# Out-projection as four more outputs of the second feed-forward's program

## The reference, cut to what matters

```
xn = _layernorm(x)                                       # x is the first layer's result
x = x + attn(xn) + ffn(xn)
# attn: 16 heads of 32
out = softmax(causal(q @ k.T / sqrt(32))) @ v            # before: o_parked, not yet divided by the sums
out = out.reshape(b, l, d) @ W_out.T + b_out
# ffn
h = silu(xn @ w_gate) * (xn @ w_up)                      # 2048 wide
h_sparse = of each four neighbours the two largest by magnitude, the others 0
return h_sparse @ w_down
```

## Time and profile before

| | us |
|---|---|
| median of 3 runs | 1831.02 (1829.15 to 1831.48) |
| the profiled execution | 1828.41 |
| its span | 1826.6 |
| PE busy | 1721.3 (94%) |
| DVE busy | 1052.3 (58%) |
| POOL busy | 242.9 (13%) |
| mean granted clock of PE | 0.975 |

### The profile page before, as it was taken

The page is one execution under the profiler, slowest core; times in us unless marked ns, Lnnn a source line. Parts: engine busy times, 40 slices in busy tenths (PEclk is TensorE's granted clock), DMA queues, the critical chain, the costliest instruction groups (busy, mean ns, idle before and its releaser), DMA issues. The chain is left out here.

```text
span 1826.6 us, 24866 instructions
## 1 busy us (share of the span) xinstructions
PE 1721.3 (94%) x8428; PEld 1383.6 (76%) x8428; DVE 1052.3 (58%) x1800; ACT 748.2 (41%) x1548; POOL 242.9 (13%) x200
## 2 busy tenths in 40 slices
PE   6999999999999989979998999948899999999997
PEld 4767877878878768857776777737688888888885
DVE  4422556455423532569997999946457556555653
ACT  4412223223113422269998999932322212222121
POOL 3001202101200030200000000036203203203200
PEclk9999999999999989989999999979899999999998
DMA  7200211110100149623454444272201100101011
GB/s 282 91 9 0 70 35 47 29 41 24 35 18 35 46 181 282 253 85 103 122 134 136 128 122 123 60 244 70 93 1 35 35 1 35 34 0 34 11 46 46
DMA packets 63434, 145.12 MB, mean 79 GB/s; under 512 B 8153, under 2 KB 16729, under 8 KB 61666
## 3 DMA queue, kind: packets, MB, share of 16 engines
q1 hardware_dynamic: 63330, 143.84, 24.8%
HBM read 97.67 MB, written 46.14 MB: 79 GB/s over the span
## 5 line engine op out<-in xcount | busy, mean ns | idle before, releaser
L1781 DVE TENSOR_TENSOR pt_lo<-p_turn,pt_hi 128x512 fp32r<-128x512 f32 (+3 forms) x384 | 201.3, 551 | 25.1 <-ACT pt_hi L1756 17.7
L1774 DVE TENSOR_REDUCE row_top<-p_score 128x1 f32<-128x128 f32 (+7 forms) x256 | 189.8, 751 | 20.8 <-PE p_score L1708 20.5
L1748 ACT ACTIVATE prob<-p_score,row_top 128x128 f32<-128x128 f32 (+7 forms) x256 | 189.7, 744 | 8.0 <-DVE row_top L1774 5.9
L1756 ACT ACTIVATE pt_hi<-p_turn 128x512 fp32r<-128x512 f32 (+3 forms) x384 | 182.0, 493 | 12.4 <-issue 4.8
L1719 PE MATMUL p_turn<-ident,prob 128*128 128x128 f32 x1152 | 183.3, 278 | 3.5 <-DVE pt_lo L1781 3.3
L1227 DVE TENSOR_TENSOR hid<-hid,p_up 128x512 f32<-128x512 f32 x64 | 44.0, 688 | 222.7 <-PE p_up L704 207.0
L1734 PE MATMUL p_o<-pt_hi,v 128*128 128x512 f32 (+3 forms) x384 | 149.2, 396 | 3.8 <-ACT o_both L1764 3.1
L1719 PEld LDWEIGHTS p_turn<-ident,prob 128*128 128x128 f32 x1152 | 133.4, 142 | 17.4 <-DVE pt_lo L1781 4.1
L1706 PE MATMUL p_score<-stack 128*128 128x512 f32 (+3 forms) x384 | 129.7, 393 | 14.0 <-PEq L53 7.0
L294 DVE TENSOR_TENSOR ff_hid<-ff_hid,ff_p_up 128x512 f32<-128x512 f32 x64 | 43.9, 686 | 162.2 <-PE ff_p_up L183 161.1
L974 ACT ACTIVATE hid<-p_gate 128x512 f32<-128x512 f32 x64 | 38.3, 598 | 221.9 <-PE p_gate L704 221.8
(11 more groups left out here) (249 smaller groups left out, 3963.2 us busy)
## 6 DMA issues: line engine op xcount, KB each, us to landing
stack<-qk_parked SPq DMA_DIRECT2D x256, 128.0 KB, 3.9
qk_parked<-qk SPq DMA_DIRECT2D x16, 1024.0 KB, 3.9
raw<-in_wgu SPq DMA_DIRECT2D x32, 256.0 KB, 2.7
v_parked<-v_out SPq DMA_DIRECT2D x16, 512.0 KB, 6.0
v<-v_parked SPq DMA_DIRECT2D x8, 1024.0 KB, 9.1
o_parked<-o_both SPq DMA_DIRECT2D x64, 128.0 KB
o<-o_parked SPq DMA_DIRECT2D x8, 1024.0 KB, 8.9
ff_raw_gu<-in_wgu SPq DMA_DIRECT2D x16, 512.0 KB, 3.8
```

Of the source, the lines that this page charges most:

```text
L1748: act.activation(prob[r // QB][:, h % 2, r % QB, 0:width_of(r)], p_score[:, r % 2, 0:width_of(r)], ACT.Exp, bias=top[:, r:r + 1], accum_ou ...
L1756: act.activation(pt_hi[:, (BL * h + j) % PT, c0:W], p_turn[:, (BL * h + j) % TB, c0:W], ACT.Copy).then_inc(rounded, 1)
L1774: dve.tensor_reduce(top[:, r:r + 1], p_score[:, r % 2, 0:width_of(r)], AX_X, ALU.max, negate=True).then_inc(topped, 1)
L1781: dve.tensor_tensor(pt_lo[:, slot, c0:W], p_turn[:, (BL * h + j) % TB, c0:W], pt_hi[:, slot, c0:W].bitcast(F32), ALU.subtract).then_inc(sp ...
```

## The change

`project_out` and `feed_forward` are replaced by one function, `layer_end`, one phase.

- It starts with the gate and up products. The weights come in pieces of 256 KB through a ring of four (`e_raw`); POOL splits all of them, 12 pieces a group, the rounding as a `tensor_scalar`. The loops are written out.
- POOL makes the 16 additions of the bias row behind the 12 pieces of group 0. `res` is loaded between the raw pieces.
- `total` is inverted at once, turned by two transposes, copied by ACT and written to DRAM (`inv_parked`).
- `h_hi` has two copies, `h_lo` lies over `hid`'s two, and the banks of `p_out` are released one by one.
- Behind unit 15 there are units 16 to 19: the out-projection's quarters. Their buffers lie over `x_hi`, `x_lo` and the gate and up weights, so loads, sums and the splits of `wo` wait for the last up product. The inverse of the sums is loaded as a tile as large as the quarter (`inv_b`), in 16 DMAs that repeat a row over 32 partitions, so both inputs of the division lie in SBUF.
- Outputs 15, 17 and 19 use the banks of `p_gate` and `p_up`.

The diff, cut:

```diff
-def feed_forward(nc, tag, wgu, wd, x_hi, x_lo, res, sparse, out):
...
-def project_out(nc, o_dram, total, ident, wo, v_bias, row, parked, res):
...
+def layer_end(nc, t, x_at, total, ident, x_hi, x_lo, o_dram, inv_dram, parked, out):
+    UNITS = TT * NG
+    J = W // P
+    RING = 4
...
+        size = 4 * NC * W
+        o_raw = [nc.alloc_sbuf_tensor_at(f"o_raw{i}", [P, QUADS, 2, W], F32, offset=x_at + 2 * i * size) for i in range(2)]
+        inv_b = [nc.alloc_sbuf_tensor_at(f"inv_b{i}", [P, QUADS, W], F32, offset=x_at + (4 + i) * size) for i in range(2)]
+        wo_hi = nc.alloc_sbuf_tensor_at("wo_hi", [P, QUADS, D], F32R, offset=x_at + 6 * size)
+        wo_lo = nc.alloc_sbuf_tensor_at("wo_lo", [P, QUADS, D], F32R, offset=x_at + 7 * size)
+        o_hi = [nc.alloc_sbuf_tensor_at(f"o_hi{i}", [P, QUADS, W], F32R, offset=gu_at + i * size) for i in range(2)]
+        o_lo = [nc.alloc_sbuf_tensor_at(f"o_lo{i}", [P, QUADS, W], F32R, offset=gu_at + (2 + i) * size) for i in range(2)]
...
+        def bank(u, j):
+            if u < UNITS - 1 or (u - UNITS) % 2 == 0:
+                return p_out[:, j]
+            return (p_gate if j < 2 else p_up)[:, j % 2]
...
+            spread = inv_dram.rearrange("(m i h) n -> m h i n", i=J, h=4)
+            def load_raw(k):
+                if k >= RING:
+                    sp.wait_ge(raw_split, k - RING + 1)
+                g, i = divmod(k, 12)
+                if g == NG:
+                    src = t["wo"][:, i]
+                elif i < 8:
+                    src = t["wgu1"][g, i // 2][:, i % 2].rearrange("p k m -> p (k m)")
+                else:
+                    src = t["wd1"][g, i - 8]
+                sp.dma_start(raw[:, k % RING], src).then_inc(raw_in[k % RING], 16)
+            def load_res(q):
+                a = slice(J * q, J * q + J)
+                sp.dma_start(res[:, a], old[:, a]).then_inc(res_in[q], 16)
+            def load_o(q):
+                if q >= 2:
+                    sp.wait_ge(o_split, QUADS * (q - 1))
                 for half in range(2):
+                    sp.dma_start(o_raw[q % 2][:, :, half], o_dram[:, half, :, q * W:(q + 1) * W].rearrange("q p t -> p q t"))\
+                        .then_inc(o_in[q % 2], 16)
+                for quad in range(QUADS):
+                    for h in range(4):
+                        to = inv_b[q % 2][E * h:E * h + E, quad].rearrange("p (i n) -> p i n", i=J)
+                        sp.dma_start(to, spread[TT * quad + q, h:h + 1].to_broadcast([E, J, P])).then_inc(inv_in[q % 2], 16)
...
+            for k in range(RING + 1, 12):
+                load_raw(k)
+                if k % 2 == 0:
+                    load_res(k // 2 - 3)
+            load_res(3)
+            for k in range(12, 12 * NG + QUADS):
+                load_raw(k)
+            sp.wait_ge(inv_out, 16)
+            sp.wait_ge(up_done, NC * UNITS)
+            for q in range(2):
+                load_o(q)
+            for q in range(TT):
+                if q >= 1 and q + 1 < TT:
+                    load_o(q + 1)
+                for j in range(0, J, 2):
+                    a = slice(J * q + j, J * q + j + 2)
+                    sp.wait_ge(added, J * (UNITS + q) + j + 2)
+                    sp.dma_start(rows[:, a], res[:, a]).then_inc(stored[q], 16)
...
+            def split(k, hi, lo):
+                pool.wait_ge(raw_in[k % RING], 16 * (k // RING + 1))
+                pool.tensor_scalar(hi, raw[:, k % RING], 1.0, 0.0, ALU.mult, ALU.add).then_inc(step.up(), 1)
+                pool.wait_ge(step.sem, step.n)
+                pool.tensor_tensor(lo, raw[:, k % RING], hi.bitcast(F32), ALU.subtract).then_inc(raw_split, 1)
+            for g in range(NG):
+                for c in range(NC):
+                    if g:
+                        pool.wait_ge(up_done, NC * (TT * g - 1) + c + 1)
+                    for j in range(2):
+                        split(gu_item(g, c, j), gu_hi[:, c, j].rearrange("p k m -> p (k m)"),
+                              gu_lo[:, c, j].rearrange("p k m -> p (k m)"))
+                if g:
+                    pool.wait_ge(out_done, J * TT * g)
+                for c in range(NC):
+                    split(d_item(g, c), d_hi[:, c], d_lo[:, c])
+                if g == 0:
+                    pool.wait_ge(const_in, 32)
+                    for i in range(NT):
+                        pool.wait_ge(res_in[i // J], 16)
+                        pool.tensor_tensor(res[:, i], res[:, i], b_row[:], ALU.add).then_inc(res_biased, 1)
+            pool.wait_ge(up_done, NC * UNITS)
+            for q in range(QUADS):
+                split(wo_item(q), wo_hi[:, q], wo_lo[:, q])
+            for q in range(TT):
+                pool.wait_ge(o_in[q % 2], 32 * (q // 2 + 1))
+                o = o_raw[q % 2]
+                for quad in range(QUADS):
+                    pool.tensor_tensor(o[:, quad, 0], o[:, quad, 0], o[:, quad, 1], ALU.add).then_inc(summed, 1)
...
+            def output(u, j):
+                if u < UNITS:
+                    s = u % 2
+                    hi, lo, w_hi, w_lo = h_hi[:, s], h_lo[:, s], d_hi, d_lo
+                    if j == 0:
+                        pe.wait_ge(raw_split, d_item(u // TT, NC - 1) + 1)
+                        pe.wait_ge(lo_done, NC * u + NC)
+                    if u == UNITS - 1:
+                        pe.wait_ge(hid_done, NC * UNITS)
+                    elif u:
+                        pe.wait_ge(added, J * (u - 1) + j + 1)
+                else:
+                    q = u - UNITS
+                    hi, lo, w_hi, w_lo = o_hi[q % 2], o_lo[q % 2], wo_hi, wo_lo
+                    if j == 0:
+                        pe.wait_ge(raw_split, wo_item(QUADS - 1) + 1)
+                        pe.wait_ge(o_split, QUADS * (q + 1))
+                    pe.wait_ge(added, J * (u - 2) + j + 1)
+                rows = slice(j * P, (j + 1) * P)
+                for c in range(NC):
+                    pe.matmul(bank(u, j), hi[:, c, rows], w_hi[:, c], start=(c == 0), stop=False)
+                    pe.matmul(bank(u, j), hi[:, c, rows], w_lo[:, c], start=False, stop=False)
+                    mm = pe.matmul(bank(u, j), lo[:, c, rows], w_hi[:, c], start=False, stop=(c == NC - 1))
+                mm.then_inc(out_done, 1)
...
+            for u in range(UNITS - 1, UNITS + TT):
+                for j in range(J):
+                    output(u, j)
...
+                    act.wait_ge(kept, NC * u + c + 1)
+                    act.activation(h_hi[:, s, c], hid[:, s, c], ACT.Copy).then_inc(hi_done, 1)
...
+            def add(u):
+                for j in range(J):
+                    dve.wait_ge(out_done, J * u + j + 1)
+                    r = res[:, J * (u % TT) + j]
+                    if u < TT:
+                        dve.wait_ge(res_biased, J * u + j + 1)
+                    dve.tensor_tensor(r, r, bank(u, j), ALU.add).then_inc(added, 1)
+            def divide(q, quad):
+                o = o_raw[q % 2][:, quad, 0]
+                dve.wait_ge(inv_in[q % 2], 16 * 4 * QUADS * (q // 2 + 1))
+                dve.wait_ge(summed, QUADS * q + quad + 1)
+                dve.tensor_tensor(o, o, inv_b[q % 2][:, quad], ALU.mult).then_inc(divided, 1)
...
+            def prepare(q):
+                divide(q, 0)
+                for quad in range(1, QUADS):
+                    divide(q, quad)
+                    keep_rest(q, quad - 1)
+                keep_rest(q, QUADS - 1)
+            dve.reciprocal(total[:, :], total[:, :]).then_inc(inverted, 1)
+            for u in range(UNITS):
+                unit(u)
+                if u:
+                    add(u - 1)
+            for q in range(TT):
+                prepare(q)
+                add(UNITS - 1 + q)
+            add(UNITS + TT - 1)
...
-            phase(nc, project_out, o_dram, total, ident, t["wo"], t["v_bias"], t["bo"], parked, res)
-            phase(nc, feed_forward, "ff1", t["wgu1"], t["wd1"], x_hi, x_lo, res, True, out)
+        phase(nc, layer_end, t, at, total, ident, x_hi, x_lo, o_dram, inv_dram, parked, out)
```

More of the change, by code:

```diff
@@ L1819, in _ @@
             old = parked.rearrange("(n p) d -> p n d", p=P)
-            for t in range(TT):
-                if t >= 2:
-                    sp.wait_ge(o_split, QUADS * (t - 1))
-                for half in range(2):
-                    sp.dma_start(o[:, t % 2, :, half], o_dram[:, half, :, t * W:(t + 1) * W].rearrange("q p t -> p q t"))\
-                        .then_inc(o_loaded[t % 2], 16)
-                if t == 0:
-                    sp.dma_start(raw[:], wo).then_inc(w_loaded, 16)
-                    sp.dma_start(bias[:], v_bias).then_inc(b_loaded, 16)
-                    sp.dma_start(b_row[:], row.to_broadcast([P, D])).then_inc(b_loaded, 16)
-                sp.dma_start(res[:, BLK * t:BLK * t + BLK], old[:, BLK * t:BLK * t + BLK]).then_inc(res_loaded[t], 16)
+            rows = out.rearrange("(n p) d -> p n d", p=P)
@@ L1862, in _ @@
[L1862 to L1872 removed]
```

(25 more changed lines are left out.)

462 lines of the change are left out of this document (125 added, 337 removed).

## The result

| | before | after |
|---|---|---|
| median of 6 runs, us | 1829.55 (1827.82 to 1831.48) | 1837.94 (1836.51 to 1841.14) |
| span of the profiled execution, us | 1826.6 | 1836.5 |
| mean granted clock of TensorE | 0.975 | 0.972 |

The account below looks back on a forecast made before the run. TensorE, busy 94% of the span, was taken to bound the kernel, so only its idle or slow stretches count. Terms -79.5 + 16.8 + 5.4 + 68.2 - 1.8 = +9.1 gave a median of 1840 us, range 1812 to 1855.

Parts of the forecast that it names:

- Term 2: First selection, unit 0: GpSimd's bias adds take turns with VectorE's chain, so TensorE idles and returns at half clock; +16.8 us.
- Term 3: Before output 15: GpSimd's splits of wo and first sums take turns with VectorE's last selection, so it starts later; +5.4 us.
- term 4: Four out-projection outputs at the end; the last two wait for loads queued behind stores and for their preparation; +68.2 us.
- Term 1: Start of the phase: gate and up loads stand first, so the first gate product comes at 1205.4 instead of 1284.94; -79.5 us.
- (b): No change: only four-byte instructions, nine of 18, take turns with GpSimd; term 2 is 10.9, time 1830.5 us; chance 0.13.
- Term 5: End of the kernel: one add instead of four stands behind the last matmul; -1.8 us.
- (a): Faster: GpSimd's adds fall into VectorE's gaps and the engines don't hinder each other; -24.4 us, 1807; chance 0.12.
- (c): Faster: the first selection alone goes free because the bias adds come behind its chain; -7.7 us, 1823; chance 0.10.
- (d): Slower: loads of the inverses cost 0.8 us each, +18.7, 1850; decided by SP bursts over some 11 us; chance 0.10.
- The likeliest case: The forecast itself, all terms within a few us, own range 1833 to 1848 us; chance 0.55.

Follow-up runs that it names:

- the kernel with both edits: Changed kernel with GpSimd's bias adds spread behind later selections and SyncE's loads of quarter q + 2 issued before quarter q's store; 1796.65 us, 0.9818 of before.
- the placed one: Both those edits, plus other SBUF places so that quarters 0 and 1 load and wo is split before output 15, each quarter's sums held back; 1784.74 us.
- the placed kernel with 4 loads: The placed one with each quarter's inverses brought in 4 transfers instead of 16; 1788.71 us, 0.9771 of before.

## Why the prediction was right, point by point

The forecast was 1840.0, the time 1837.94; the medians differ by 8.4, and the span of the profiled execution grew by 9.9 where the sum said 9.1. The mechanism was right: one start saved, and four places where TensorE waits. That the sum is so near is in part luck: terms 2 and 3 were 2.7 too high, term 4 was 3.7 too low, and term 4 had a wrong reason.

- Term 1, -79.5: 1205.33 against 1284.94 is -79.6. The first piece was split by 1205.3 (0.62 and 1.26 from 1203.32), as worked out.
- Term 2, +16.8: 13.4 of idling (14.89 less 1.48) and 2.2 for the clock, since the last hid product of the unit 15 comes 64.0 sooner instead of 79.6: +15.6. Turns of 0.9 on 15 instructions were a little too many and too cheap: 13 met an add and cost 0.94 to 1.10 each.
- The rule of the Trainium skill (SBUF — State Buffer, section SBUF: two separate sides), by which VectorE with two SBUF inputs and GpSimd shut each other out for a whole instruction, decided rival (b) rightly: the trace agrees, bf16 instructions with two SBUF inputs took 1.37 to 1.48 beside GpSimd and 0.42 without. With the rule for four-byte inputs alone the term would have been 10.9.
- Term 3, +5.4: +3.9. From `top` to the first `e_h_lo` it is 16.4 us where before had 7.7. So the splits and the first four sums cost 8.7, foreseen 8.4 of the 10.2; the second quarter's sums started at 1746.77, just after the chain, and cost nothing here.
- Term 4, +68.2: last matmul's end 1831.83 less 1746.18, less 13.7, is +71.9, the term that was most mis-sized. Idle stretches of 12.36 and 12.04, not 10.0 and 9.0. The date at which the loads are issued was right for quarter 2 (25.4 us from output 15's start, foreseen 25.7). What was mis-sized is the step from there to the landing of the inverses: 18 issues of 0.5 and 2.7 to land, 11.7, measured 15.4 and 15.6. The preparation behind it was priced at 8.1 and took 6.7, which hides a part. And the reason was wrong. I put the date down to SyncE's burst of 16 (8.0, plus 2.7 to land). The bursts took 10.0 and 10.6, yet with one of 2.8 the stretches were no shorter, and with neither burst nor inverses only 1.7 to 1.8 shorter. What is left of the wait is the load of 2 MB, which I had given no time of its own: 10.5 to 12.8 us from issue. That the 11.7 is near those figures is chance.
- Term 5, -1.8: -1.85.
- Sum: -79.6 + 15.6 + 3.9 + 71.9 - 1.85 = +9.95.
- Rivals: (a) and (b) fall by the rows of VectorE beside GpSimd; (c) by the selection's rows: the adds started at 1228.06, ahead of it, and the run with the adds spread shows what (c) would have been, 1824.9 against the 1823 worked out. (d) falls by its own mark: the bursts took 10.0 and 10.6, under the 11 that it asked for.

The likeliest case had its marks as foretold: a first gate product near 1205, an idle stretch of 12 to 18, 8 to 14 before output 15, none before 16 and 17. The last two stretches were over the 8 to 11 given, and the bursts over the 8.

What stays open is why the load of 2 MB takes 10.5 us. The run without inverses in 1771:1791, in 40 slices of 0.5 us, DMA share in tenths and GB/s, then what was moved:

```profile
DMA  0000059977967799799999751000000000000000
GB/s 4 0 0 0 0 213 365 340 148 197 250 147 115 201 246 238 242 336 385 410 414 414 307 229 49 0 0 0 0 0 0 0 0 0 0 0 0 0 0 0
DMA packets 1337, 2.62 MB, mean 131 GB/s; under 512 B 56, under 2 KB 56, under 8 KB 1337
```

After 1.5 us at 213 to 365 come 4.5 us at 115 to 250 GB/s and 2.5 at 336 to 414, with the DMA engines 6 to 9 tenths busy in the first and 9 in the second. The 2.62 MB are more than the load's 2.10: the other 0.52 is the store of finished rows that is issued at 1772.81, right ahead of it. In the run with the loads two quarters ahead, quarter 2's load has no store ahead of it and quarter 3's has one (issues on SyncE and the sums that wait for the landing):

```profile
1754.81 0.94 SPq L1620 DMA_DIRECT2D o_raw<-o_parked  x2
...
1770.10 1.45 SPq L1620 DMA_DIRECT2D o_raw<-o_parked  x2
```

```profile
1764.69 5.04 POOL L1688 TENSOR_TENSOR o_raw<-o_raw 128x512 f32<-128x512 f32 x4 [13.87 <-DMA o_raw<-o_parked]
...
1782.78 5.47 POOL L1688 TENSOR_TENSOR o_raw<-o_raw 128x512 f32<-128x512 f32 x4 [13.05 <-DMA o_raw<-o_parked]
```

They land after 9.9 and 12.7 us, each with its inverses beside it. So a store right ahead may be a part of the 10.5, but not most of it, since 9.9 pass without one. What slows the rest, and the store by itself, was not tried.

## What to carry to other kernels

When a phase is folded into the program of the one before, its preparation has to fold in too: list for each engine what it must do before the first new output, and find the time, the buffer and the place in the queue for it ahead of that output; a wait put in to keep two engines apart only moves the cost when the work behind it has no slack. A load that stands in a queue behind a store is as late as the store: issue it before. Work on GpSimd beside a chain of short VectorE instructions with two SBUF inputs is priced by their count, here about 1 us for each one of 128x512, and belongs where TensorE doesn't wait for that chain.

## What the runs showed of the hardware that I had not expected

- bf16 instructions of 0.42 us lose more in proportion than four-byte ones of 0.69: both pay about the same microsecond (1.37 to 1.48, and 1.63 to 1.78). GpSimd's adds lose little: 1.52, against 1.26 in the last twelve of the run with the adds spread.
- Making 4 DMAs of 16 took 7.2 us off SyncE, and the bytes landed 1.5 us later, not sooner (1.2 in the last quarter). Why is open.
- Idle stretches of 5.75 us and more, in before and in every run looked at, were followed by 5 us at 0.50 to 0.68 of the clock. Behind the short ones it went either way. Here the 5 us behind the 2.31 of the kernel with both edits, and then those behind the 2.94 of the placed one:

```profile
1781.00:1786.00 5.00, 5.00 (x15) 4.01 (x16) 2.77 (x5) 0.00 (x0) 0.00 (x0) 0.66 0.56 210
```

```profile
1767.00:1772.00 5.00, 4.96 (x22) 4.14 (x23) 3.02 (x5) 0.00 (x0) 0.00 (x0) 1.00 0.56 210
```

The first had 9.59 us of idling some 50 us earlier, the second 0.93. That does not tell the two apart: the placed kernel with 4 loads had 0.94 there too, and got 0.66 behind its 3.46. What does was not tried.
